# A twelve-stage network in one kernel: two stage joints reordered, retention on two PSUM banks with its state on GpSimd, indirect row loads limited to two in flight

## The reference

```python
x = x + 0.5 * L0_ffn(ln(x));  x = x + L0_attn(ln(x));  x = x + 0.5 * L0_ffn(ln(x))
x = x + 0.5 * L1_ffn(ln(x));  x = x + L1_attn(ln(x));  x = x + 0.5 * L1_ffn(ln(x))
x = x + 0.5 * L2_ffn(ln(x));  x = x + L2_attn(ln(x));  x = x + 0.5 * L2_ffn(ln(x))
x = x + 0.5 * L3_ffn(ln(x));  x = x + L3_attn(ln(x));  x = x + 0.5 * L3_ffn(ln(x))
```

## Time and profile before

| | |
|---|---|
| median of 3 runs | 2124.52 us (2124.52 to 2133.64) |
| the profiled execution | 2124.77 us, of which the span of the trace is 2123.0 us |
| mean granted PE clock | 0.978 of full |
| PE busy | 1987.1 us (94%) |
| DVE, ACT, POOL busy | 1468.1 us (69%), 1012.4 us (48%), 260.6 us (12%) |
| chain that ended last | PE 83%, DVE 7%, ACT 5%, issue 3% |
| first sorted blocks, second | about 645 to 714 us, about 1402 to 1471 us |
| time mix | ends about 1653 us |
| retention | about 1898 to 1991 us, then the last mixture stage |

### The profile page before, as it was taken

How to read it: one execution, slowest core, us unless ns; L and a number is a source line. 1 busy time by engine, 2 the same in 40 slices (tenths; PEclk the granted TensorE clock), 3 DMA queues, 4 the chain that set the end, 5 groups by cost and what they waited for, 6 DMA issues and landing times.

```text
span 2123.0 us, 38784 instructions
## 1 busy us (share of the span) xinstructions
PE 1987.1 (94%) x13148; PEld 1242.4 (59%) x13148; DVE 1468.1 (69%) x4162; ACT 1012.4 (48%) x1898; POOL 260.6 (12%) x408
## 2 busy tenths in 40 slices
PE   7999999998999899999999998999997899998898
PEld 3523333333678556666666665778674677774576
DVE  6679999994566556666666666466658545877786
ACT  4347767776334355555555553345433333342233
POOL 2252212111027200000000000073000000000000
PEclk9989999999999999999999999999999999999999
DMA  6210000000027400000000000256100000000000
GB/s 238 32 63 26 26 23 28 23 23 24 16 74 220 123 1 1 1 0 0 0 0 0 0 1 1 75 164 206 51 1 0 1 1 1 1 1 2 1 1 21
DMA packets 62912, 78.07 MB, mean 37 GB/s; under 512 B 18954, under 2 KB 36638, under 8 KB 62017
## 3 DMA queue, kind: packets, MB, share of 16 engines
q1 hardware_dynamic: 57536, 67.18, 10.1%
q0 software_dynamic: 4672, 8.99, 1.7%
q10 hardware_dynamic: 576, 0.26, 0.1%
HBM read 64.14 MB, written 10.88 MB: 35 GB/s over the span
## 4 chain that ended last, share of the span: by engine, by line
PE 83%; DVE 7%; ACT 5%; issue 3%; DMA 1%; SPq 1%; ACTq 0%; POOL 0%; DVEq 0%; POOLq 0%
PE ps L455 13%; PE ps L434 12%; PE ps L1033 7%; PE ps L1067 6%; PE ps L2644 6%; PE ps L2607 6%; PE ps L2628 5%; PE ps L1050 4%; PE ps L835 3%; PE ps L846 3%; PE ps L2081 2%; PE ps L1017 2%; PE ps L1079 2%; ACT arena L1170 1%; PE ps L1039 1%
## 5 line engine op out<-in xcount | busy, mean ns | idle before, releaser
L455 PEld LDWEIGHTS ps<-l_w,arena 128*128 128x128 f32 x2560 | 335.4, 192 | 161.2 <-issue 144.1
L2894 DVE TENSOR_REDUCE arena<-ps 128x1 f32<-128x512 f32 x512 | 325.9, 684 | 40.9 <-PE ps L2607 40.9
L455 PE MATMUL ps<-l_w,arena 128*128 128x128 f32 x2560 | 339.3, 276 | 6.0 <-ACT arena L506 5.0
L434 PE MATMUL ps<-xnT,l_w 128*128 128x512 f32 x640 | 330.5, 599 | 3.0 <-ACT xnT L265 3.0
L2799 ACT ACTIVATE arena<-ps 128x1024 f32<-128x1024 f32 x256 | 252.6, 1022 | 102.1 <-PE ps L2628 101.4
L1233 DVE TENSOR_REDUCE arena<-ps 128x1 f32<-128x128 f32 (+7 forms) x256 | 178.6, 749 | 158.8 <-PE ps L1039 158.7
L588 DVE SCALAR_TENSOR_TENSOR x<-ps,comb,x 128x128 f32<-128x128 f32 x576 | 162.2, 344 | 151.6 <-PE ps L455 149.8
L506 ACT ACTIVATE arena<-ps,l_b 128x512 f32<-128x512 f32 x192 | 131.7, 687 | 216.2 <-PE ps L434 215.7
L1178 ACT ACTIVATE arena<-ps 128x512 f32<-128x512 f32 (+1 forms) x192 | 85.4, 489 | 231.5 <-PE ps L1050 231.4
L1170 ACT ACTIVATE arena<-ps,arena 128x128 f32<-128x128 f32 (+7 forms) x256 | 187.0, 745 | 13.2 <-DVE arena L1233 13.2
L2607 PE MATMUL ps<-arena 72*128 72x512 bf16 x512 | 184.3, 389 | 1.8 <-DVE arena L2894 1.1
...
## 6 DMA issues: line engine op xcount, KB each, us to landing
...
```

The costliest lines, as they stand in the source:

```text
L434: pe.matmul(k.ps[:, n % 2, :], w.w1[:, e, f * P:(f + 1) * P], k.xnT[:, g * GW:(g + 1) * GW], start=True, stop=True).then_inc(s.hidden_mm.s ...
L455: ins = pe.matmul(k.ps[:, 2 + e % 4, j * P:(j + 1) * P], w.h[:, n % 2, j * P:(j + 1) * P], w.w2[:, e, f, :], start=(f == 0 and j == 0), st ...
L2894: dve.tensor_reduce(s.nm2[:, place, qt, half:half + 1], k.ps[:, bank, :], AX.X, ALU.max, negate=True)\
```

## The change

It has four parts.

1. Behind the time mix: PE's output(1, 3) is no longer the mix's last step. It stands in the next mixture stage behind unit 1 (`leftover`), and the wait at unit 0 is for 7 instead of 8 additions. On DVE, add(1, 2) stands ahead of states(1, 3).
2. Behind retention: DVE does the next stage's front of group 0 right behind its first addition to x, not behind the fourth. The next stage waits at unit 0 for all four additions, and its matmuls of zeros are 12 instead of 40. The output matmuls use banks 5, 2, 3, 4.
3. In retention: output and outer product alternate between banks 6 and 7, and PE's order per chunk is state, scores of the next chunk, outer product, the 16 small matmuls. The wait for ACT's copy ahead of the state is for the chunk before the last one; the wait for the last one stands ahead of the outer product. The outer product is copied to SBUF by ACT, and the state is made on POOL by three instructions of 128x128 (S * gC, KV * block, their sum) instead of two on DVE. Counting semaphores of the projections become one (`proj`), without another order.
4. In the sorted blocks: each indirect load from the third on waits until the load two before it has landed, and PE waits per pack of 4 blocks instead of per 8 (four semaphores, `gathered[b % GT]`, take the place of the old ones).

```diff
@@ -293,7 +293,7 @@
         self.y_mm = k.counted("moe_y_mm", groups * self.units)
         self.y_used = k.counted("moe_y_used", groups * NE)
         self.sparse = Sparse(k, w) if sparse else None
-        self.mixed = None
+        self.mixed, self.filler, self.leftover = None, 40, None
 
     TURN, OWN_TURN, OWN_GLOW, OWN_RATIOS = 2, 2, 6, ((0, 4), (1, 2))
     LEAD_TURN, LEAD_GLOWS = 10, {1: (0, 12), 2: (1, 1), 3: (1, 2)}
@@ -435,8 +435,7 @@
                   start=True, stop=True).then_inc(s.hidden_mm.sem, 1)
 
     if not s.early and not s.lead:
-        if s.mixed is None:
-            keep_busy(pe, k, s.idle_bank, 40)
+        keep_busy(pe, k, s.idle_bank, s.filler)
         front_turn(pe, k, s.norm, 0)
     hidden(0)
     if s.solo and s.gate == "gelu":
@@ -448,7 +447,7 @@
             hidden(n + 1)
         pe.wait_ge(s.hidden.sem, s.hidden.at(n + 1))
         if n == 0 and s.mixed is not None:
-            pe.wait_ge(s.mixed, 2 * NG)
+            pe.wait_ge(*s.mixed)
         if f == 0 and s.y_used.at(g * NE + e - 3) > 0:
             pe.wait_ge(s.y_used.sem, s.y_used.at(g * NE + e - (2 if s.lead and n < 3 * nf else 3)))
         for j in range(GT):
@@ -456,6 +455,8 @@
                             w.w2[:, e, f, :], start=(f == 0 and j == 0), stop=(f == nf - 1),
                             skip_group_check=True)
         ins.then_inc(s.y_mm.sem, 1)
+        if n == 1 and s.leftover is not None:
+            mix_output(pe, k, s.leftover, 1, NG - 1)
         if g == 0:
             for late in range(max(s.early, 1), NG):
                 if i == s.turn_unit(late):
...
@@ -612,7 +613,7 @@
     TOKENS = TS * P
     CHOICES = 2 * TS
     BLOCKS = (2 * TOKENS + NE * (P - 1)) // P
-    RING, XRING = 6, 3
+    RING, XRING, FLIGHT = 6, 3, 2
     PACKS = (BLOCKS + GT - 1) // GT
     PREFIX_UNIT, INDEX_UNIT = 10, 18
     BACK = (8192, 12288)
...
@@ -714,9 +715,12 @@
     pool.wait_ge(s.stored.sem, s.stored.at(16 * NG))
     pool.wait_ge(s.listed.sem, s.listed.at(s.INDEX))
     for b in range(s.BLOCKS):
+        if b >= s.FLIGHT:
+            landed = s.gathered[(b - s.FLIGHT) % GT]
+            pool.wait_ge(landed.sem, landed.at(16 * ((b - s.FLIGHT) // GT + 1)))
         pool.indirect_dma_start(s.xg[:, b, :], None, s.w.x_rows,
                                 bass.IndirectOffsetOnAxis(ap=s.src[:, b:b + 1], axis=0))\
-            .then_inc(s.gathered[b // (2 * GT)].sem, 16)
+            .then_inc(s.gathered[b % GT].sem, 16)
     for b in range(s.BLOCKS):
         pool.wait_ge(s.y_out.sem, s.y_out.at(b + 1))
         pool.indirect_dma_start(s.w.y_rows, bass.IndirectOffsetOnAxis(ap=s.dst[:, b:b + 1], axis=0), s.yb[:, b, :], None)\
@@ -814,9 +818,8 @@
 def sparse_tensor(pe, k, m, s):
 
     def rows_in(c):
-        if c % 2 == 0:
-            come = s.gathered[c // 2]
-            pe.wait_ge(come.sem, come.at(16 * min(2 * GT, s.BLOCKS - c * GT)))
+        for come in s.gathered[:s.pack(c)]:
+            pe.wait_ge(come.sem, come.at(16 * (c + 1)))
         if c >= 2:
             pe.wait_ge(s.xT_out.sem, s.xT_out.at(c - 1))
         for j in range(s.pack(c)):
@@ -1320,6 +1323,21 @@
         return 6 + g % 2 if i == 0 or g < 2 else 2 + 3 * (g % 2)
 
 
+def mix_output(pe, k, s, i, g):
+
+    w, lower, n = s.w, s.norms[1], i * NG + g
+    pe.wait_ge(s.y, n + 1)
+    if i == 0 and g >= 2:
+        pe.wait_ge(s.o_used, n - 1)
+    if i == 1 and g < 2:
+        pe.wait_ge(lower.ready.sem, lower.ready.at(g + 3))
+    for j in range(GT):
+        t = g * GT + j
+        ins = pe.matmul(k.ps[:, s.o_bank(i, g), j * P:(j + 1) * P], s.prod[:, t * P:(t + 1) * P], w.wo[:, i, :],
+                        start=True, stop=True)
+    ins.then_inc(s.o_mm, 1)
+
+
 def mix_tensor(pe, k, s):
     w, lower = s.w, s.norms[1]
     pe.wait_ge(w.loaded, w.loads)
...
@@ -1478,8 +1481,8 @@
     add(1, 1)
     front_stats(dve, st, k, 0, 1)
     front_rows(dve, k, s.nxt.norm, 0)
+    add(1, 2)
     states(1, 3)
-    add(1, 2)
     add(1, 3)
     k.stats_given = False
 
...
@@ -1530,6 +1534,21 @@
 def retention_pool(pool, k, s):
     pool.wait_ge(*s.free)
     pool.memset(s.vm[:, :, :], 0.0).then_inc(s.cleared, 1)
+    w, steps = s.w, 0
+    pool.wait_ge(w.loaded, w.loads)
+    for n in range(NT):
+        u = s.updates(n)
+        if n % s.CHUNKS == s.CHUNKS - 1:
+            continue
+        pool.wait_ge(s.outer_out, u + 1)
+        if n % s.CHUNKS == 0:
+            pool.tensor_tensor(s.S, s.KV, w.block[:, :], ALU.mult).then_inc(s.state, 1)
+            continue
+        pool.tensor_scalar(s.S, s.S, w.gC[:, 0:1], None, ALU.mult).then_inc(s.masking, 1)
+        pool.tensor_tensor(s.KV, s.KV, w.block[:, :], ALU.mult).then_inc(s.masking, 1)
+        steps += 2
+        pool.wait_ge(s.masking, steps)
+        pool.tensor_tensor(s.S, s.S, s.KV, ALU.add).then_inc(s.state, 1)
 
 
 def retention_tensor(pe, k, s):
@@ -1575,21 +1594,25 @@
     scores(0)
     for n in range(NT):
         c = n % s.CHUNKS
+        bank = 6 + n % 2
+        if n >= 2:
+            pe.wait_ge(s.o_out, n - 1)
+        if c:
+            pe.wait_ge(s.state, s.updates(n))
+            pe.matmul(k.ps[:, bank, 0:P], s.S, s.qd[:, n * P:(n + 1) * P], start=True, stop=False,
+                      skip_group_check=True)
+        if n + 1 < NT:
+            scores(n + 1)
         if n >= 1:
             pe.wait_ge(s.o_out, n)
-        if c:
-            pe.wait_ge(s.state, s.updates(n))
-            pe.matmul(k.ps[:, 6, 0:P], s.S, s.qd[:, n * P:(n + 1) * P], start=True, stop=False,
-                      skip_group_check=True)
         if c < s.CHUNKS - 1:
-            pe.matmul(k.ps[:, 7, 0:P], s.kd[:, n, :], s.v[:, n, :], start=True, stop=True).then_inc(s.outer, 1)
-        if n + 1 < NT:
-            scores(n + 1)
+            pe.matmul(k.ps[:, 13 - bank, P:2 * P], s.kd[:, n, :], s.v[:, n, :], start=True, stop=True,
+                      skip_group_check=True).then_inc(s.outer, 1)
         pe.wait_ge(s.vm_out, n + 1)
         pe.wait_ge(s.decayed, 2 * n + 2)
         for m in range(4):
             for q in range(4):
-                ins = pe.matmul(k.ps[32 * q:32 * q + 32, 6, 0:P],
+                ins = pe.matmul(k.ps[32 * q:32 * q + 32, bank, 0:P],
                                 s.vm[:, n % 2, P * m + 32 * q:P * m + 32 * q + 32], s.pT[n % 2][:, 4 * q + m, :],
                                 start=(c == 0 and m == 0), stop=(m == 3), tile_position=(0, 32 * q),
                                 skip_group_check=True)
...
@@ -1630,11 +1653,21 @@
         act.activation(dst.rearrange("p m (q z) -> p m q z", z=32)[:, :, :, 0:8],
                        s.v[:, n, :].rearrange("p (q m d) -> p m q d", m=4, d=8), ACT.Copy).then_inc(s.vm_out, 1)
 
+    def outer(n):
+        u = s.updates(n)
+        act.wait_ge(s.outer, u + 1)
+        if u:
+            act.wait_ge(s.state, u)
+        act.activation(s.KV, k.ps[:, 7 - n % 2, P:2 * P], ACT.Copy).then_inc(s.outer_out, 1)
+
     spread(0)
     spread(1)
+    outer(0)
     for n in range(NT):
         act.wait_ge(s.o_mm, 4 * (n + 1))
-        act.activation(s.oT[:, n * P:(n + 1) * P], k.ps[:, 6, 0:P], ACT.Copy).then_inc(s.o_out, 1)
+        act.activation(s.oT[:, n * P:(n + 1) * P], k.ps[:, 6 + n % 2, 0:P], ACT.Copy).then_inc(s.o_out, 1)
+        if n + 1 < NT and (n + 1) % s.CHUNKS < s.CHUNKS - 1:
+            outer(n + 1)
         if n + 2 < NT:
             spread(n + 2)
 
...
@@ -1681,15 +1714,6 @@
             dve.tensor_tensor(s.pT[n % 2][:, 8 * half:8 * half + 8, :],
                               k.ps[:, s.half(i), :].rearrange("p b (h l) -> p (b h) l", l=P),
                               every(w.mask, 8), ALU.mult).then_inc(s.decayed, 1)
-        if c < s.CHUNKS - 1:
-            dve.wait_ge(s.outer, s.updates(n) + 1)
-            if c == 0:
-                dve.tensor_tensor(s.S, k.ps[:, 7, 0:P], w.block[:, :], ALU.mult).then_inc(s.state, 1)
-                dve.wait_ge(s.state, s.updates(n) + 1)
-            else:
-                st.done(dve.tensor_tensor(s.KV, k.ps[:, 7, 0:P], w.block[:, :], ALU.mult))
-                dve.scalar_tensor_tensor(s.S, s.S, w.gC[:, 0:1], s.KV, ALU.mult, ALU.add).then_inc(s.state, 1)
-                dve.wait_ge(s.state, s.updates(n) + 1)
         if n >= GT and n % GT == 0:
             part_stats(n // GT - 1)
     st.done(part_stats(NG - 1))
@@ -1724,11 +1748,14 @@
     for g in range(NG):
         dve.wait_ge(s.y_mm, g + 1)
         x = k.x[:, g * GT:(g + 1) * GT, :]
-        dve.tensor_tensor(x, k.ps[:, g, :].rearrange("p (j d) -> p j d", d=D), x, ALU.add)\
+        dve.tensor_tensor(x, k.ps[:, s.Y_BANKS[g], :].rearrange("p (j d) -> p j d", d=D), x, ALU.add)\
             .then_inc(s.y_used, 1)
         dve.wait_ge(s.y_used, g + 1)
-        ins = token_stats(dve, k, g)
-    st.done(ins)
+        st.done(token_stats(dve, k, g))
+        if g == 0:
+            front_stats(dve, st, k, 0, 1)
+            front_rows(dve, k, s.nxt.norm, 0)
+    k.stats_given = False
 
 
 
@@ -3079,9 +3106,11 @@
```

(6 more changed lines are left out.)

54 lines of the change are left out of this document (21 added, 33 removed).

## The result

The changed kernel took 2134.81 us (median of 15 runs, 2130.17 to 2140.95) beside 2128.94 of the kernel before on the same chip (15 runs, 2124.52 to 2136.23): a ratio of 1.003, 95% interval 1.0017 to 1.0042. Timed again in a1_changed it had 1.0027 (1.0012 to 1.0042). So it is 6 us slower: real, and within the 0.5% called "same". The profiled execution took 2130.17 us, its span is 2128.4.

The account below looks back on a forecast made before the run. PE, busy 94% of the span, was taken to bound the kernel. Terms -5.7 + 4.7 + 3.5 + 0.2 = +2.7 on the profiled 2124.77 gave 2127.5, forecast as 2127 us; range for 8 in 10: 2114 to 2136.

Parts of the forecast that it names:

- Joint behind retention: After retention: transposes start 6.0 us earlier and the logits copy just fits, -5.7 us (weak end -4, strong end -6.1).
- Loop: Retention: the state's chain through ACT and POOL makes a chunk 3.87 us, 0.60 more than before; +4.7 us in all.
- The named sign: Retention: PE waits before the state's product for POOL's last instruction (L1551), about 0.8 us, 12 times, with chunks of 3.9.
- The two rivals in which the state is hidden or nearly so: Retention's loop: POOL's three instructions under 0.5 us, total 2114.5 (12%); or at 0.84 us, total 2120 (5%).
- the first rival: Retention's loop: POOL's three instructions under 0.5 us, 2.7 us per chunk, -8 in place of +4.7, total 2114.5 (12%).
- What the Trainium skill's figure would have made of it: Retention's loop: by an estimated 0.28 us for 128 columns on POOL, the loop would come to -2.6 us.
- Mix joint: Behind the time mix: an earlier start is given back because the moved output delays DVE; +3.5 us, bounds -0.5 and +6.
- The named waits: Behind the mix: PE idles about 4 us before the second transposes, DVE some 5 us ahead of its last addition.
- the branch in which the block starts at half clock: Behind the mix: clock at 0.50 until 1652.4 puts the moved output 2.2 us later, at 1658.4.
- The rival in which the joint opens: Behind the mix: DVE reaches the logits copy before PE, -3.6 us instead of +3.5, total 2120 (10%).
- Sorted blocks: Paced row loads: last loads end later but PE does not wait; +0.2 us, bounds -2 and +5.
- The rival in which pacing starves the stores: Sorted blocks: at 3.3 us per load beside weights, stores end 11 us later, total 2145 (9%).

Follow-up runs that it names:

- a1_changed: The changed kernel itself, timed again on a third chip where the kernel before took 2127.77 us: 2135.07 us, ratio 1.0027.
- j1_joint: The kernel before with only the opened joint behind retention, on a second chip where the kernel before took 2191.28 us: 2185.4 us, ratio 0.9974.
- p2: The changed kernel with PE's outer product ahead of the next chunk's scores again, on the second chip: 2158.49 us, ratio 0.985 to the kernel before.
- r2_mix: The changed kernel with the mix joint of the kernel before: 2128.38 us, ratio 1.0008 to the kernel before.
- m1_earlier: The changed kernel with the mix's last four output products ahead of the block's first unit, on the second chip: 2168.51 us, ratio 0.9892 to the kernel before.
- b1_best: The changed kernel with mix outputs ahead of unit 0, state decay ahead of the chain, outer product before scores: 2119.62 us, 0.9953 of the kernel before.
- b3_unpaced: b1_best with unpaced row loads in both sorted blocks: 2117.95 us, ratio 0.9948 to the kernel before.
- r3_rows: The changed kernel with unpaced row loads in both sorted blocks: 2137.84 us, ratio 1.0046 to the kernel before.
- b4_stores: b1_best with the row stores paced too, each waiting for the landing of the second before it: 2161.47 us, ratio 1.014 to the kernel before.

## Why the prediction was right or wrong

- **The time.** 2127 was forecast and 2134.8 measured, within 2114 to 2136 near its upper end, and "same" was the likeliest class. It is above this case's own 2120 to 2133 by 2. The forecast's picture held: one joint gives, loop and other joint take. Both costs were sized too small, by 3.0 and some 1.1, both in the same direction, so nothing cancelled.
- **Joint behind retention, -5.7 forecast.** Measured -5.5, step by step: 16.0 from the first addition to the transposes of group 1 (15.8 forecast), the logits copy in time by 0.21. j1_joint confirms it alone, 5.9 us. (The end of the twelve zeros adds up to 1990.49, not 1990.45, which changes nothing.)
- **Loop, +4.7 forecast.** Measured +7.7; this is the term that was mis-sized. POOL's three instructions were priced at 1.50 and took 1.55, so that price holds. The 0.20 more a chunk (4.07 for 3.87) is 0.05 from them, 0.05 and 0.11 in the hops from ACT to POOL (0.10) and from POOL to PE (0.15), and 0.09 from the outer product's start to the end of ACT's copy (0.81 for 0.72), less 0.10 in the state product, behind whose start the scores came after 0.39. Ten chunks are full ones with a wait: 2.0. The other 0.9 is in the three chunks without a wait, which took 2.88 to 2.96 instead of 2.64, since state product and outer product take PE 0.42 each from start to start where I had 0.22. The named sign came: PE waits for L1551 12 times, 1.1 each instead of 0.8. The two rivals in which the state is hidden or nearly so failed with this kernel, and p2 shows a condition that I had not seen: not only a POOL under 0.5 or 0.84, but also the outer product ahead of the scores. Its price was wrong too, -3.1 against the kernel before where the first rival had -8, because PE's own four steps took 2.96 in the changed kernel's first chunk, not 2.7, and the wait for ACT's copy makes it 3.04. I had counted the scores into the chain and did not ask what they did there.
- **What the Trainium skill's figure would have made of it** (GPSIMD Engine Reference, section 3.1, an estimated 0.28 us for 128 columns): the measured 0.45 to 0.46 per tensor_tensor sides with the earlier trace rows: the estimate is too low by 0.17 to 0.18.
- **Mix joint, +3.5 forecast.** Measured 4.5 to 4.7 by the traces and by r2_mix. The named waits are there, larger: DVE idle 7.4 (forecast some 5), PE idle 4.32 ahead of the second transposes (about 4), the half clock behind it 1.7 (1 to 2). Up to the second transposes the loss is 2.8, the upper end of +0.5 to +2.8: the branch in which the block starts at half clock held (0.50 from 1646 to 1649), and I had taken a middle of both. The rival in which the joint opens (-3.6) failed. With the products in another place, m1_earlier avoids the loss, but it gains 0.8 at most on the kernel before.
- **Sorted blocks, +0.2 forecast.** By b1_best against b3_unpaced the parts differ by 0.0005 of the time, and by the changed kernel against r3_rows by 0.0016 the other way, each within overlapping intervals, so this was right on the chips of that speed, to some 5 us. The gaps between loads came as named, 0.6 in the mean up to 650 and 1.3 from there. My reason for zero, bytes and landings alone, missed that ACT and DVE could stand while row loads are issued, which cost 26 to 29 us on the slower chip; no row of the kernel before showed such a wait. The rival in which pacing starves the stores did not occur with loads. b4_stores is its mechanism, with the stores themselves paced.
